# Forming 1 / (row sum of exponentials) as a power on GpSimd instead of a reciprocal on VectorE

## The chip, the cores and the metric

The kernel runs on one core of one Trainium2 chip. The core has five engines that run beside each other and meet only at semaphores: TensorE (PE, with its weight load PEld), VectorE (DVE), ScalarE (ACT), GpSimd (POOL) and SyncE (SP, which here only issues DMAs). The metric is the device time of one launch in microseconds; three runs of the kernel before took 1795.38 to 1799.1 us, median 1796.7.

## The reference

A gated cross attention is followed by a gated mixture of experts, for 8 batches of 512 tokens with 256 channels and a context of 1601 rows. What matters here is the attention. Its softmax runs over the query axis (`axis=2`), so each of the 1601 context rows is normalised over the 512 queries of its head:

```python
attn = jnp.einsum('bhnc,bhlc->bhnl', qh * scale, kh)
attn = jax.nn.softmax(attn, axis=2)
attn = attn / jnp.sum(attn, axis=-1, keepdims=True)
out = jnp.einsum('bhnl,bhlc->bhnc', attn, vh)
...
x = x + jnp.tanh(g_xattn[0]) * _L0_xattn_ref(_layernorm(x, axis=-1), ctx_1024, ctx_1024, ...)
x = x + jnp.tanh(g_ffn[0]) * _L0_ffn_ref(_layernorm(x, axis=-1), L0_ffn_router_w, L0_ffn_w1, L0_ffn_w2)
```

With the context rows on the partitions, the softmax's sum is a sum along a partition's own row, and its reciprocal can be multiplied into the values instead of into the probabilities.

## The kernel before

The attention goes batch by batch. A batch has 52 steps (`STEPS`): 4 groups of 4 heads, and for each group 13 tiles (`LT`) of 128 context rows (the last has 65). A step has two units of two heads. All 416 steps of the 8 batches do the same:

- TensorE makes the scores of a unit, two matmuls of 128x512 (`unit_scores`, line 732), into one of 3 slots of two PSUM banks. A slot is free again when ScalarE has done the exponentials of three units ago.
- VectorE takes the negated maximum over the queries (line 1114, one TENSOR_REDUCE per unit).
- ScalarE takes the exponentials, one ACTIVATE per head (line 934), and has their row sums written to `z`, 128x4 for a step, in a ring of 4 (`RING`). Its semaphore is `exp_done`.
- VectorE forms `rz` = 1 / `z` (`reciprocals`, line 1100). It does so for step s-1 behind the second maximum of step s.
- GpSimd multiplies the values of the step, a 128x4x17 tile (16 channels of 4 heads and a column of ones), with `rz` into `vz` (`weigh_values`, line 1337). In its program this stands at the head of step s for step s-1.
- TensorE multiplies `vz` with the exponentials into `acc` (`weigh`, line 745). In its program this stands three steps later (`LAG` = 3), between the scores of two units, so a late `vz` holds the scores behind it.

Each engine works through a fixed program in order. Around these steps a table, `FILL_AT`, places one "fill" at a step: the projections of the next batch, its layer normalisation, and the residual, normalisation and routing of the batch before (its "tail"). On GpSimd the fills are: for each chunk of the projected keys and queries, the middle part in the chunk's step (line 1389) and the low part one step later (line 1381); in steps 13 to 16 the tail's normalisation, `one_over_deviation` (lines 1306 and 1308) and six `by_row` (line 1314); in steps 17 to 20 the same for the next batch's input, with four `by_row`; and in steps 44 to 51 one indirect DMA each (line 1397). Chunks stand at steps 1, 3, 11, 13, 15, 17, 24, 26 (keys) and 30, 32 (queries). `one_over_deviation` has a power in it already: line 1308 raises a 128x4 tile to -1/2.

Batch 0 has no tail and batch 7 has no next batch. After the last batch, `last` goes on with the last routing, and some 500 us of expert blocks follow that neither form nor use `rz`. The profiled execution starts batch 4's exponentials at 634.5 us and those of batch 5 at 785.8 us; "step 13" below is step 13 of batch 4.

Of the kernel before, what the change touches and what calls it, by code (L numbers as in the profile page):

```python
# [207 lines left out]
def rows_of(lt):  # L208
    return min(P, L - lt * P)


def attention_and_routing(nc, ctx, block, keep, x, ctx_t, g_xattn, g_ffn, wq_t, wk_t, wv_t, wo_t, router_t,
# [8 lines left out]
    def sb(name, shape, dt=F32):  # L221
        return ctx.enter_context(nc.sbuf_tensor(name, shape, dt))
# [51 lines left out]
    rstd2 = sb("rstd2", [P, 2, NT])  # L274
    minus_half = sb("minus_half", [P, NT])
    prob = sb("prob", [P, 3, NT, E])
    one_hot = sb("one_hot", [P, 2, NT, E])
# [117 lines left out]
    ROUTE_STEPS, PLACE_STEPS = 25, 6  # L395
    DVE_SETUP = 7 + 2 * E

# [547 lines left out]
    def _(dve):  # L945
        for tile, value in ((v_ones[0][:, :, :, DH], 1.0), (v_ones[1][:, :, :, DH], 1.0), (vz[:, :, :, :], 0.0), (minus_half[:, :], -0.5),
                            (zero[:, :], 0.0), (seen[:, :], 0.0), (ones_e[:, :], 1.0)):
            dve.memset(tile, value).then_inc(dve_setup, 1)
# [146 lines left out]

        def reciprocals(b, s):

            r = rows_of(s % LT)
            dve.wait_ge(exp_done, 2 * (b * UNITS + 2 * s + 2))
            dve.reciprocal(rz[0:r, s % RING, :], z[0:r, s % RING, :]).then_inc(rz_ready, 1)  # L1100

        def take_acc(b, g):
# [3 lines left out]
        def run(it):  # L1106
            b = it.b
            for s in range(STEPS):
                for p in range(2):
# [9 lines left out]
                    if p == 1 and it.cur and s in (LT + LAG - 1, 2 * LT + LAG - 1, 3 * LT + LAG - 1):  # L1119
                        take_acc(b, s // LT - 1)  # L1120
                    if p == 1 and s == 0 and it.tail:
                        reciprocals(b - 1, STEPS - 1)
                    if p == 1 and s > 0 and it.cur:
                        reciprocals(b, s - 1)
                    f = it.fill(s)
# [36 lines left out]
        def last():  # L1162
            b = B - 1
            reciprocals(b, STEPS - 1)
            dve.wait_ge(last_router_summed, 1)
# [115 lines left out]
    def _(pool):  # L1281
# [48 lines left out]
        def weigh_values(b, s):  # L1330

            g, lt = s // LT, s % LT
            r = rows_of(lt)
            pool.wait_ge(rz_ready, b * STEPS + s + 1)

            wait(pool, pv_done, b * STEPS + s - RING + 1)
            pool.tensor_tensor(vz[0:r, s % RING, :, 0:DH + 1], v_ones[b % 2][0:r, lt, g * GH:(g + 1) * GH, :],  # L1337
                               rz[0:r, s % RING, :].unsqueeze(2).to_broadcast([r, GH, DH + 1]),
                               ALU.mult).then_inc(vz_ready, 1)
# [349 lines left out]
```

## Time and profile before

| | |
|---|---|
| runs | 1796.7, 1799.1, 1795.38 us |
| profiled execution, time | 1794.36 us |
| profiled execution, first to last instruction | 1792.6 us |
| granted TensorE clock, mean | 0.996 |
| busy: TensorE, VectorE, ScalarE, GpSimd | 1703.8, 1417.2, 1283.0, 538.2 us |

The span is first to last instruction; the time of the execution is 1.8 us longer. Engines are named PE, PEld, DVE, ACT, POOL and SP in the rows, and L1100 is line 1100 of the kernel. A group's row gives its busy time, the mean duration of one, then the idle time of the engine just ahead of these instructions with what ended it. Instructions overlap on an engine's pipeline: the start of the next can be earlier than the end of the one before, and what one costs in a full stretch is the distance from start to start.

### The profile page before, as it was taken

Reading aid. Unit: us, or ns where it says so; the run is one execution under the profiler, and the core shown is the slowest. Engines: PE = TensorE matmul, PEld = TensorE weight load, DVE = VectorE, ACT = ScalarE, POOL = GpSimd, SP = SyncE. Lnnn points to the kernel's source line nnn. Section 1 sums busy time; section 2 is a strip of 40 time slices with the busy share of each in tenths; the row PEclk is TensorE's granted clock in tenths of the full one; section 3 lists DMA queues with packets and bytes.
Section 4 is the critical chain, followed back from the end, with each engine's and each line's share of the span. In section 5 each row is a group of like instructions: output and inputs, shape, how many; then the busy total and the mean of one; then the engine's idle time right before and its main releaser. Section 6 shows DMA issues by size and latency. Waiting matters only on the chain.

```text
span 1792.6 us, 31795 instructions
## 1 busy us (share of the span) xinstructions
PE 1703.8 (95%) x10074; PEld 918.3 (51%) x10074; DVE 1417.2 (79%) x2293; ACT 1283.0 (72%) x3653; POOL 538.2 (30%) x821
## 2 busy tenths in 40 slices
PE   8999999999999999999999999889999999999997
PEld 5233334333333433333333342225899999999997
DVE  7998999999999999999999999997344444444442
ACT  5999999999999999999999999996111111111111
POOL 3331252352343225235223422213122222222222
PEclk9999999999999999999999999999999999999999
DMA  8546226414712721551371163419222222222221
GB/s 231 139 121 183 66 70 158 129 40 123 187 47 62 198 72 52 158 154 40 102 187 51 51 172 75 154 52 326 67 37 35 36 37 35 38 35 35 36 37 27
DMA packets 128247, 172.90 MB, mean 96 GB/s; under 512 B 14496, under 2 KB 105760, under 8 KB 128128
## 3 DMA queue, kind: packets, MB, share of 16 engines
q1 hardware_dynamic: 113152, 150.51, 30.8%
q0 software_dynamic: 14144, 20.44, 6.6%
q8 instruction: 54, 0.88, 0.2%
q14 instruction: 65, 0.53, 0.1%
q10 hardware_dynamic: 832, 0.53, 0.1%
HBM read 117.96 MB, written 53.47 MB: 96 GB/s over the span
## 4 chain that ended last, share of the span: by engine, by line
ACT 40%; PE 30%; DVE 20%; issue 7%; DMA 2%; POOL 1%; SPq 0%; POOLq 0%; DVEq 0%; ACTq 0%
ACT w_all L934 37%; DVE negmax L1114 14%; PE scores L1507 14%; PE scores L1520 13%; ACT w_all L879 1%; ACT parts L870 1%; DVE resid L1009 1%; DMA out<-row_t,gate_token 1%; PE spare L1497 1%; DVE rz L1100 1%; PE scores L732 1%; PE spare L593 1%; DVE x L1025 1%; DVE stats L1133 1%; DVE stats L1143 0%
## 5 line engine op out<-in xcount | busy, mean ns | idle before, releaser
L934 ACT ACTIVATE w_all<-scores,negmax 128x512 f32<-128x512 f32 (+1 forms) x1664 | 1128.9, 778 | 19.9 <-DVE negmax L1114 15.4
L1114 DVE TENSOR_REDUCE negmax<-scores 128x2 f32<-128x1024 f32 (+1 forms) x832 | 1001.9, 1215 | 53.8 <-PE scores L732 47.4
L732 PE MATMUL scores<-q_stack,w_all 128*128 128x512 bf16 (+1 forms) x1664 | 532.9, 385 | 42.1 <-ACT w_all L934 34.3
L934 ACT ACTIVATION_READ_ACCUMULATOR w_all<-scores,negmax 128x1 f32 (+1 forms) x1664 | 495.2, 298 | 0.0
L745 PE MATMUL acc<-w_all,vz 128*32 128x512 f32 (+1 forms) x3328 | 443.7, 605 | 0.0
L732 PEld LDWEIGHTS scores<-q_stack,w_all 128*128 128x128 bf16 (+1 forms) x1664 | 136.8, 99 | 575.2 <-ACT w_all L934 514.6
L1553 ACT ACTIVATE projections<-scores 128x512 f32<-128x512 f32 x142 | 84.8, 597 | 445.8 <-PE scores L1507 440.2
L1337 POOL TENSOR_TENSOR vz<-w_all,rz 128x68 f32<-128x68 f32 (+1 forms) x416 | 124.5, 299 | 776.3 <-DVE rz L1100 751.0
L1507 PEld LDWEIGHTS scores<-row_t,q_stack 128*128 128x128 f32 x2272 | 264.4, 192 | 7.0 <-issue 2.0
L1507 PE MATMUL scores<-row_t,q_stack 128*128 128x128 f32 x2272 | 265.6, 275 | 1.9 <-DVE row_t L1580 1.9
L1520 PE MATMUL scores<-room,projections 128*128 128x256 f32 x1136 | 256.8, 379 | 0.0
L1633 POOL DMA_INDIRECT out<-row_t,gate_token x71 | 120.3, 1694 | 407.9 <-DVE row_t L1593 374.3
L1520 PEld LDWEIGHTS scores<-room,projections 128*128 128x128 f32 x1136 | 210.4, 190 | 25.7
L1586 DVE COPY gate_token<-parts 128x2 f32<-128x2 f32 x71 | 12.0, 169 | 186.3 <-DMA out<-row_t,gate_token 186.3
L745 PEld LDWEIGHTS acc<-w_all,vz 128*32 128x32 f32 (+1 forms) x3328 | 65.6, 108 | 138.1 <-issue 121.9
L593 PE MATMUL spare<-w_all,projections 128*128 128x400 f32 (+1 forms) x228 | 97.7, 511 | 10.2 <-DVE resid L1009 10.2
L1593 DVE TENSOR_SCALAR row_t<-scores,gate_token 128x256 f32<-128x256 f32 x71 | 34.4, 484 | 88.0 <-PE scores L1520 88.0
L601 PE MATMUL spare<-projections,w_all 128*128 128x256 f32 (+1 forms) x400 | 103.1, 381 | 0.1
L1570 DVE COPY q_stack<-w_all 128x2048 f32 x71 | 86.9, 1225 | 6.4 <-issue 1.8
L1575 DVE COPY room<-w_all 128x2048 f32 x71 | 86.5, 1218 | 0.0
L601 PEld LDWEIGHTS spare<-projections,w_all 128*128 128x128 f32 (+1 forms) x400 | 73.6, 186 | 19.8 <-ACT w_all L879 3.3
L1100 DVE RECIPROCAL rz<-z 128x4 f32<-128x4 f32 (+1 forms) x416 | 69.7, 167 | 2.1 <-ACT w_all L934 2.1
(215 smaller groups left out, 1048.9 us busy)
## 6 DMA issues: line engine op xcount, KB each, us to landing
w_all<-k_parts SPq DMA_DIRECT2D x248, 200.1 KB, 3.5
w_all<-in_w SPq DMA_DIRECT2D x16, 1024.0 KB, 10.0
q_stack<-q_parts SPq DMA_DIRECT2D x248, 64.0 KB, 3.3
k_parts<-parts SPq DMA_DIRECT2D x42, 300.0 KB, 2.9
w_all<-in_ctx_t SPq DMA_DIRECT2D x7, 1601.0 KB, 7.1
parts<-routed SPq DMA_DIRECT2D x71, 129.0 KB
q_parts<-parts SPq DMA_DIRECT2D x14, 384.0 KB, 3.9
routed<-pad_row SPq DMA_DIRECT2D x8, 645.0 KB
```

The lines of the kernel that those rows point to most:

```text
L593: mm = pe.matmul(bank[:, 0:KCOLS[c + 1] - KCOLS[c]], wk_sb[:, k, m * P:(m + 1) * P], ctx_sb[:, k, KCOLS[c]:KCOLS[c + 1]], start=(k == 0), ...
L601: mm = pe.matmul(bank[0:r, (lt % 2) * D:(lt % 2 + 1) * D], ctx_sb[:, k, lt * P:lt * P + r], wv_sb[:, k, :], start=(k == 0), stop=(k == KC ...
L732: mm = pe.matmul(scores[0:r, 2 * (u % SLOTS) + j % 2, :], k_stacks[g][:, j, lt * P:lt * P + r], q_stack[:, g, j, :], start=True, stop=True)
L745: mm = pe.matmul(acc[32 * j:32 * j + 32, :], vz[0:r, s % RING, j, :], probs[0:r, s % RING, j, :], start=(lt == 0), stop=(lt == LT - 1))
L934: act.activation(probs[0:r, s % RING, j, :], scores[0:r, 2 * (u % SLOTS) + j % 2, :], ACT.Exp, bias=negmax[0:r, u % 4, j % 2:j % 2 + 1], a ...
L1100: dve.reciprocal(rz[0:r, s % RING, :], z[0:r, s % RING, :]).then_inc(rz_ready, 1)
L1114: dve.tensor_reduce(negmax[0:r, u % 4, :], scores[0:r, 2 * (u % SLOTS):2 * (u % SLOTS) + 2, :], AX.X, ALU.max, negate=True).then_inc(negma ...
L1337: pool.tensor_tensor(vz[0:r, s % RING, :, 0:DH + 1], v_ones[b % 2][0:r, lt, g * GH:(g + 1) * GH, :], rz[0:r, s % RING, :].unsqueeze(2).to_ ...
L1507: mm = pe.matmul(ps_hidden[:, slot * BANKS + h // HB, (h % HB) * BLK:(h % HB + 1) * BLK], w1_sb[:, slot, k * HID + h * P:k * HID + (h + 1) ...
L1520: mm = pe.matmul(ps_y[:, slot, 0:D], hidden[:, slot, h * BLK:(h + 1) * BLK], w2_sb[:, slot, h * D:(h + 1) * D], start=(h == 0), stop=(h == ...
L1570: dve.tensor_copy(w1_sb[:, slot, :], w1_all[:, bass.ds(e * (KC * HID), KC * HID)]).then_inc(w1_ready, 1)
L1633: pool.indirect_dma_start(out=out, out_offset=bass.IndirectOffsetOnAxis(gate_token[:, slot, 1:2].bitcast(U32), 0), in_=result[:, slot, :], ...
```

## The change

The power -1 of `z` is taken on GpSimd, with `tensor_tensor` and `ALU.pow` against a new 128x4 tile of -1, just ahead of the multiplication that uses it. `rz_ready`, which VectorE raised, is now raised by GpSimd and waited for by GpSimd itself. VectorE's `reciprocals` and its 415 calls inside the batches go; the last step of the last batch alone keeps a VectorE reciprocal, behind one added wait.

```diff
--- before.py
+++ after.py
@@ -273,6 +273,7 @@
     mv2 = sb("mv2", [P, NT, 2])
     rstd2 = sb("rstd2", [P, 2, NT])
     minus_half = sb("minus_half", [P, NT])
+    minus_one = sb("minus_one", [P, GH])
     prob = sb("prob", [P, 3, NT, E])
     one_hot = sb("one_hot", [P, 2, NT, E])
     tmp = sb("tmp", [P, 2, NT, E])
@@ -393,7 +394,7 @@
 
     passed_sp, passed_dve, passed_pool = (sem(f"passed_{e}") for e in ("sp", "dve", "pool"))
     ROUTE_STEPS, PLACE_STEPS = 25, 6
-    DVE_SETUP = 7 + 2 * E
+    DVE_SETUP = 8 + 2 * E
 
     def load_w1(eng, e):
         eng.dma_start(w1_all[:, e * KC * HID:(e + 1) * KC * HID].rearrange("p (k h) -> p k h", k=KC),
@@ -943,7 +944,7 @@
 
     @block.vector
     def _(dve):
-        for tile, value in ((v_ones[0][:, :, :, DH], 1.0), (v_ones[1][:, :, :, DH], 1.0), (vz[:, :, :, :], 0.0), (minus_half[:, :], -0.5),
+        for tile, value in ((v_ones[0][:, :, :, DH], 1.0), (v_ones[1][:, :, :, DH], 1.0), (vz[:, :, :, :], 0.0), (minus_half[:, :], -0.5), (minus_one[:, :], -1.0),
                             (zero[:, :], 0.0), (seen[:, :], 0.0), (ones_e[:, :], 1.0)):
             dve.memset(tile, value).then_inc(dve_setup, 1)
         for e in range(E):
@@ -1093,12 +1094,6 @@
             chain(dve.tensor_scalar(token[:, :], token[:, :], float(N), None, ALU.add))
             yield
 
-        def reciprocals(b, s):
-
-            r = rows_of(s % LT)
-            dve.wait_ge(exp_done, 2 * (b * UNITS + 2 * s + 2))
-            dve.reciprocal(rz[0:r, s % RING, :], z[0:r, s % RING, :]).then_inc(rz_ready, 1)
-
         def take_acc(b, g):
             dve.wait_ge(pv_done, b * STEPS + (g + 1) * LT)
             dve.tensor_copy(o_acc[:, :], acc[:, :]).then_inc(acc_taken, 1)
@@ -1118,10 +1113,6 @@
                         take_acc(b - 1, G - 1)
                     if p == 1 and it.cur and s in (LT + LAG - 1, 2 * LT + LAG - 1, 3 * LT + LAG - 1):
                         take_acc(b, s // LT - 1)
-                    if p == 1 and s == 0 and it.tail:
-                        reciprocals(b - 1, STEPS - 1)
-                    if p == 1 and s > 0 and it.cur:
-                        reciprocals(b, s - 1)
                     f = it.fill(s)
                     if f and f[0] not in ("v", "own_v", "x_turn") and p == (f[0] in ("q", "k")):
                         take(it, *f)
@@ -1161,7 +1152,10 @@
         dve.wait_ge(constants, 1)
         def last():
             b = B - 1
-            reciprocals(b, STEPS - 1)
+            dve.wait_ge(rz_ready, B * STEPS - 1)
+            dve.wait_ge(exp_done, 2 * B * UNITS)
+            r, at = rows_of(LT - 1), (STEPS - 1) % RING
+            dve.reciprocal(rz[0:r, at, :], z[0:r, at, :]).then_inc(rz_ready, 1)
             dve.wait_ge(last_router_summed, 1)
             dve.tensor_copy(router_sum[:, :], spare[:, 0:E]).then_inc(last_router_sum_taken, 1)
             dve.wait_ge(pv_done, B * STEPS)
@@ -1331,6 +1325,9 @@
 
             g, lt = s // LT, s % LT
             r = rows_of(lt)
+            if s < STEPS - 1 or b < B - 1:
+                pool.wait_ge(exp_done, 2 * (b * UNITS + 2 * s + 2))
+                pool.tensor_tensor(rz[0:r, s % RING, :], z[0:r, s % RING, :], minus_one[0:r, :], ALU.pow).then_inc(rz_ready, 1)
             pool.wait_ge(rz_ready, b * STEPS + s + 1)
 
             wait(pool, pv_done, b * STEPS + s - RING + 1)
```

On GpSimd, batch 1, from the end of step 12 to step 15 (65 rows is the last, short tile of a group; batches 2 to 6 have the same program). Before:

```order
L1337 TENSOR_TENSOR vz<-w_all,rz 65x4x17
L1306 TENSOR_SCALAR rstd<-mv 128x4
L1308 TENSOR_TENSOR rstd<-rstd,minus_half 128x4
L1314 TENSOR_TENSOR routed_rows<-x,mv 128x2x256
L1389 TENSOR_TENSOR parts<-resid,zero 128x401
L1337 TENSOR_TENSOR vz<-w_all,rz 128x4x17
L1314 TENSOR_TENSOR routed_rows<-x,mv 128x2x256
L1314 TENSOR_TENSOR routed_rows<-routed_rows,rstd 128x2x256
L1381 TENSOR_TENSOR parts<-resid,parts 128x401
L1337 TENSOR_TENSOR vz<-w_all,rz 128x4x17
```

and now:

```order
L1330 TENSOR_TENSOR rz<-z,minus_one 65x4
L1334 TENSOR_TENSOR vz<-w_all,rz 65x4x17
L1300 TENSOR_SCALAR rstd<-mv 128x4
L1302 TENSOR_TENSOR rstd<-rstd,minus_half 128x4
L1308 TENSOR_TENSOR routed_rows<-x,mv 128x2x256
L1386 TENSOR_TENSOR parts<-resid,zero 128x401
L1330 TENSOR_TENSOR rz<-z,minus_one 128x4
L1334 TENSOR_TENSOR vz<-w_all,rz 128x4x17
L1308 TENSOR_TENSOR routed_rows<-x,mv 128x2x256
L1308 TENSOR_TENSOR routed_rows<-routed_rows,rstd 128x2x256
L1378 TENSOR_TENSOR parts<-resid,parts 128x401
L1330 TENSOR_TENSOR rz<-z,minus_one 128x4
```

In the new rows L1330 is the power, L1334 the old L1337, L1300, L1302 and L1308 the old L1306, L1308 and L1314, and L1386 and L1378 the old L1389 and L1381. Each multiplication into `vz` has a power ahead of it, in the same place of the order; nothing else changed places.

On VectorE, batch 1, steps 11 to 13. Before:

```order
L1114 TENSOR_REDUCE negmax<-scores 65x2
L1143 BN_STATS stats<-room 128x6
L1114 TENSOR_REDUCE negmax<-scores 65x2
L1100 RECIPROCAL rz<-z 128x4
L1137 BN_AGGR mv<-stats 128x2 x4
L1114 TENSOR_REDUCE negmax<-scores 128x2
L1143 BN_STATS stats<-room 128x6
L1114 TENSOR_REDUCE negmax<-scores 128x2
L1100 RECIPROCAL rz<-z 65x4
L1009 SCALAR_TENSOR_TENSOR resid<-spare,parts 128x401
```

and now:

```order
L1109 TENSOR_REDUCE negmax<-scores 65x2
L1134 BN_STATS stats<-room 128x6
L1109 TENSOR_REDUCE negmax<-scores 65x2
L1128 BN_AGGR mv<-stats 128x2 x4
L1109 TENSOR_REDUCE negmax<-scores 128x2
L1134 BN_STATS stats<-room 128x6
L1109 TENSOR_REDUCE negmax<-scores 128x2
L1010 SCALAR_TENSOR_TENSOR resid<-spare,parts 128x401
```

L1109 is the old L1114, L1134 the old L1143, L1128 the old L1137 and L1010 the old L1009. The reciprocals are gone, and with each its wait for ScalarE; the rest stands as it stood.

## Rows read from the trace of the kernel before

**Rows 1.** The page: the chain that ended last, share of the span.
```profile
ACT 40%; PE 30%; DVE 20%; issue 7%; DMA 2%; POOL 1%; SPq 0%; POOLq 0%; DVEq 0%; ACTq 0%
```

**Rows 2.** The page, costliest groups: busy us, mean ns | idle before, releaser.
```profile
L934 ACT ACTIVATE w_all<-scores,negmax 128x512 f32<-128x512 f32 (+1 forms) x1664 | 1128.9, 778 | 19.9 <-DVE negmax L1114 15.4
L1114 DVE TENSOR_REDUCE negmax<-scores 128x2 f32<-128x1024 f32 (+1 forms) x832 | 1001.9, 1215 | 53.8 <-PE scores L732 47.4
...
L1337 POOL TENSOR_TENSOR vz<-w_all,rz 128x68 f32<-128x68 f32 (+1 forms) x416 | 124.5, 299 | 776.3 <-DVE rz L1100 751.0
...
L1100 DVE RECIPROCAL rz<-z 128x4 f32<-128x4 f32 (+1 forms) x416 | 69.7, 167 | 2.1 <-ACT w_all L934 2.1
```

**Rows 3.** Busy by stretch (from, to, length): PE, PEld, DVE, ACT, POOL; clock, DMA, GB/s.
```profile
632.00:781.00 149.00, 142.22 (x783) 50.94 (x783) 142.64 (x232) 146.34 (x431) 53.04 (x93) 1.00 0.39 109
674.50:692.80 18.30, 16.46 (x90) 5.58 (x93) 17.93 (x30) 17.72 (x53) 17.64 (x26) 1.00 0.20 66
```

**Rows 4.** Groups by form, ScalarE: steps 1 to 12 (two forms), then 24 to 51.
```profile
L934 ACT ACTIVATE w_all<-scores,negmax 128x512 f32<-128x512 f32 x45 | 30.3, 705 | 0.7 <-DVE negmax L1114 0.5
...
L934 ACT ACTIVATE w_all<-scores,negmax 65x512 f32<-65x512 f32 x4 | 2.7, 676 | 0.8 <-DVE negmax L1114 0.8
...
L934 ACT ACTIVATE w_all<-scores,negmax 128x512 f32<-128x512 f32 (+1 forms) x114 | 77.9, 810 | 0.0
```

**Rows 5.** Timeline, VectorE: start, us, engine, line; idle in brackets.
```profile
650.96 2.33 DVE L1114 TENSOR_REDUCE negmax<-scores 128x2 f32<-128x1024 f32 x2
653.21 0.17 DVE L1100 RECIPROCAL rz<-z 128x4 f32<-128x4 f32 x1
653.29 1.20 DVE L1114 TENSOR_REDUCE negmax<-scores 128x2 f32<-128x1024 f32 x1
...
701.62 1.23 DVE L1114 TENSOR_REDUCE negmax<-scores 128x2 f32<-128x1024 f32 x1 [0.20 <-PE scores L732]
```

**Rows 6.** Groups by form: the power of 128x4 on POOL, and the scatter.
```profile
L1397 POOL DMA_INDIRECT routed<-routed_rows,place x56 | 56.6, 1011 | 11.4 <-issue 11.4
...
L1308 POOL TENSOR_TENSOR rstd<-rstd,minus_half 128x4 f32<-128x4 f32 x16 | 16.6, 1038 | 1.3
```

**Rows 7.** Timeline, POOL, batch 4, from step 13.
```profile
674.51 0.30 POOL L1337 TENSOR_TENSOR vz<-w_all,rz 65x68 f32<-65x68 f32 x1 [1.71 <-DVE rz L1100]
674.77 0.23 POOL L1306 TENSOR_SCALAR rstd<-mv 128x4 f32<-128x4 f32 x1
675.08 1.04 POOL L1308 TENSOR_TENSOR rstd<-rstd,minus_half 128x4 f32<-128x4 f32 x1
676.21 1.04 POOL L1314 TENSOR_TENSOR routed_rows<-x,mv 128x512 f32<-128x512 f32 x1
677.20 0.85 POOL L1389 TENSOR_TENSOR parts<-resid,zero 128x401 bf16<-128x401 f32 x1
...
692.49 0.30 POOL L1337 TENSOR_TENSOR vz<-w_all,rz 128x68 f32<-128x68 f32 x1 [0.17 <-DVE rz L1100]
...
697.74 0.30 POOL L1337 TENSOR_TENSOR vz<-w_all,rz 128x68 f32<-128x68 f32 x1 [1.03 <-DVE rz L1100]
```

**Rows 8.** Timeline, ScalarE: last sum of step 12; one of step 23.
```profile
672.71 0.19 ACT L934 ACTIVATION_READ_ACCUMULATOR w_all<-scores,negmax 65x1 f32 x1
...
703.36 0.75 ACT L934 ACTIVATE w_all<-scores,negmax 128x512 f32<-128x512 f32 x1
```

**Rows 9.** Timeline, TensorE: weighing of steps 18 and 20, scores behind.
```profile
695.61 1.07 PE L745 MATMUL acc<-w_all,vz 128*32 128x512 f32 x8
...
699.98 1.06 PE L745 MATMUL acc<-w_all,vz 128*32 128x512 f32 x8
700.97 0.61 PE L732 MATMUL scores<-q_stack,w_all 128*128 128x512 bf16 x2
```

**Rows 10.** Busy by stretch, TensorE alone: length, busy; granted clock, DMA, GB/s.
```profile
1080.00:1088.60 8.60, 6.49 (x36) 1.00 0.37 95
1088.60:1092.00 3.40, 3.40 (x16) 0.50 0.96 253
```

## The prediction

> **What bounds the kernel now.** I read the chain of waits first, to see which engine sets the end. It gives ScalarE 40%, TensorE 30% and VectorE 20% of the span, GpSimd 1% [rows 1]; TensorE's share is largely the expert part. In the costliest groups the 1664 exponentials of ScalarE sat idle ahead for 19.9 us in all, 15.4 of it until VectorE's maxima [rows 2]. So in the attention ScalarE is nearly full, and no relief of VectorE can bring more than some 15 to 20 us. The reciprocals to be dropped are 416, 167 ns each, 69.7 us together [rows 2]. The busy time by stretch gives one batch: of 149.0 us ScalarE is busy 146.34, VectorE 142.64, GpSimd only 53.04 [rows 3]. The average hides what the second row of that group shows: from 674.5 to 692.8 us GpSimd is busy 17.64 of 18.30 us, with two normalisations and three key chunks in steps 13 to 18. That stretch comes in each of batches 1 to 6. ScalarE's groups by stretch show where it loses: 1.5 us (0.7 + 0.8) in steps 1 to 12, and nothing in steps 24 to 51 [rows 4].
>
> **What goes.** On VectorE a reciprocal costs less than its 167 ns, since it overlaps its neighbours: the second of a pair of maxima is over at 653.29, and the next begins there, with the reciprocal between; the pair without one between them took 2.33 us at 1.22 a piece, so one begins 0.11 us before the last ends [rows 5]. A reciprocal is thus worth 0.11 us of VectorE, 12 of them 1.3 us by step 12. ScalarE has 1.5 us of idle time to give back there, and part of that is held by TensorE or by a bank, not by VectorE. Bounds: 0 and 1.5 us a batch; I take 0.9, between them and nearer to the 1.3. From step 24 on ScalarE has no idle time, so the other 28 reciprocals bring nothing.
>
> **What comes.** 415 powers on GpSimd. The trace has the same operation on the same shape: line 1308, 128x4, 1038 ns, 16 times [rows 6]. In a full stretch it costs from its start at 675.08 to the next start at 676.21, which is 1.13 us [rows 7]. The scaling behind it keeps its 0.30 us, 0.26 from start to start (674.51 to 674.77), and so on an idle GpSimd `vz` is there 0.05 + 1.13 + 0.30 = 1.5 us behind the last row sum. At the head of the stretch the old path needed more: the sum ends at 672.90 [rows 8] and `vz` at 674.81 [rows 7], 1.9 us, since the reciprocal stood behind a maximum. Outside the full stretch I therefore cost the powers at nothing: a step lasts 2.87 us (149.0 / 52), and a power, a scaling and one chunk operation of 0.85 or 0.94 us are 2.3 us. With the scatter's 1.01 us in steps 44 to 51 [rows 6] they are 2.4 to 2.7 us. If that cover were gone, each step would run over by some tenths, which the three steps of lag absorb over 8 steps.
>
> The Trainium skill's Perfetto Trace Analysis (GPSIMD Engine Instruction) says not to trust the reported duration of a GpSimd instruction but the spacing of consecutive starts. Durations alone would make the seven powers below 0.6 us shorter a batch, some 4 us in all; the spacing in rows 7 is what I use.
>
> **The full stretch, step by step.** Step 12's last sum is there at 672.90 [rows 8]. Power 672.95 to 674.08, scaling to 674.34: line 1306 starts 0.43 us earlier than its 674.77 [rows 7]. From there GpSimd worked without a break up to 692.32 (692.49 less 0.17 of idle time), 17.55 us with five scalings in it. Five powers more are 5.65 us: it is done at 691.89 + 5.65 = 697.54. Then step 18: power to 698.67, `vz` at 698.97. A `by_row` of 0.99 from start to start (676.21 to 677.20), step 19 with 1.39, a `by_row`, and the power of step 20: 698.93 + 0.99 + 1.39 + 0.99 + 1.13 = 703.43, `vz` at 703.73. The row sums of these steps are no limit: step 20's scaling ran at 697.74 already [rows 7]. TensorE weighed step 18 at 695.61 and step 20 at 699.98 [rows 9]. So these come 3.4 and 3.8 us late. The other steps of the stretch end before that and are not added: lateness is one delay that grows.
>
> What of it reaches ScalarE: weighing at 703.78, scores 0.99 us later (699.98 to 700.97 [rows 9]), the maximum 0.65 us behind them (701.62 [rows 5]), 1.23 us for it, and the exponential at 706.7 us instead of 703.36 [rows 8]. That is +3.3 us. ScalarE has no idle time left afterwards to win it back. VectorE's 0.9 us moves the start of the whole sequence forward: +2.4 us a batch, and 6 x 2.4 = 14.4 us.
>
> Batches 0 and 7 have one normalisation each and no such stretch: at most a step is late by less than its slack. They keep VectorE's gain, which I put at 0.5 us for both. At the end of batch 7 the last power delays the weighing of step 50 by some 0.4 us, and the reciprocal kept on VectorE is where it was. The memset of the new tile lies ahead of the first data, nothing. Sum: 14.4 - 0.5 + 0.4 = +14.3 us. On the profiled execution's 1794.4 us (span 1792.6 and 1.8 around it) that is 1808.7; it lies 2.3 us under the median of the runs, 1796.7, and on the median it is **1811 us**, 0.8% slower.
>
> Bounds of the sum: with 1.00 us a power instead of 1.13 (a pipelined start) the lateness shrinks by 0.9, with VectorE's full 1.5 it shrinks by 0.6 more: +0.9 a batch, 1802. With nothing from VectorE and half a microsecond lost while the pipeline refills, +3.8 a batch, 1820.
>
> **Rivals.**
> 1. *The price of the power is the tile's size, and no backlog forms.* Then only VectorE's relief is left: 6 x 0.9 to 1.5 us and a little from batches 0 and 7, some 9 us: 1788. For it: 128x4 has a 17th of the elements of the scaling, which takes 0.30 us. Against it: line 1308, 16 times at 1038 ns. The Trainium skill's GPSIMD Engine Reference (Performance versus the Vector engine) gives a two-input tensor_tensor 2.6 cycles an element at 1.2 GHz; an estimate from that page for 4 elements is 9 ns on top of a fixed part, which would make this rival true. The trace does not agree where the operation is a power. It ends on the faster side if seven powers add less than some 1.3 us a batch, that is under 0.2 us each.
> 2. *The slack takes it.* TensorE is late, but scores already made feed ScalarE through, and VectorE's gain covers the rest: 1797, within 3.6 us. For it: three slots of scores. Against: the slack from maximum to exponential behind step 20's weighing is about half a microsecond, which the path above already spends.
> 3. *TensorE's clock falls in the gap.* Where the trace shows a stretch of 8.6 us with 6.49 busy, the clock granted afterwards was 0.50 for 3.4 us, which is 1.2 GHz [rows 10]. A hole of 3 us in steps 18 to 20 leaves a thinner stretch than that. In that slow stretch TensorE was busy all of 3.40 us [rows 10]; work that takes half of that at full clock is late by some 1.3 us on top, 8 us over six batches: 1819.
> 4. *GpSimd stays behind.* The backlog meets the chunks at steps 24 and 26 before it is gone, or the low parts of a chunk reach SyncE so late that ScalarE waits for a free buffer: 1 to 2 us more a batch, 1823.
>
> **How the numbers follow.** Forecast 0.60, rival 1 0.07, rival 2 0.09, rival 3 0.15, rival 4 0.09. What a measurement can tell from no change is about 0.2%, 3.6 us: 1793.1 to 1800.3. Rival 1 is the faster side with 0.07, and 0.02 of the forecast's lower end; rival 2 and 0.02 of the lower end fall within; the rest is slower: 0.09, 0.10, 0.81. The range leaves out rival 1, most of rival 2 and the far end of 4: 1799 to 1825.
>
> **What would show it.** In the profile after: the power's group on GpSimd with 415 at about 1040 ns; GpSimd busy about 107 us of a batch; VectorE's reciprocals gone and its busy time down by 69 us. TensorE's weight load for `acc` waits for `vz`, which it did for 16 us in all, with 3 us and more at a time, around steps 18 to 20 of batches 1 to 6 alone. ScalarE has an idle time of about 3 us there. A batch of 1 to 6 lasts 151.3 + 2.4 = 153.7 us from its first exponential to the next batch's (785.8 - 634.5 = 151.3 now); batches 0 and 7 stay as they are. It is wrong if batches 1 to 6 don't grow, if the waits lie in other steps, or if the clock shows 0.50 in these stretches.

## The result, and the profile after

The changed kernel took 1827.28 us (median of six runs, 1819.88 to 1829.52) against 1797.64 of the kernel before (1795.38 to 1799.1): the ratio is 1.0158, with a 95% interval of 1.0143 to 1.0173. It is slower by twice what was forecast, and 2.3 us above the range. The profiled execution took 1826.45 us with a span of 1824.7, 32.1 us more than the span before.

The page after, the chain that ended last and the groups that answer to [rows 1] and [rows 2]:

```profile
PE 41%; ACT 28%; POOL 11%; DVE 11%; issue 7%; DMA 2%; POOLq 0%; SPq 0%; DVEq 0%; ACTq 0%
...
L935 ACT ACTIVATE w_all<-scores,negmax 128x512 f32<-128x512 f32 (+1 forms) x1664 | 1128.7, 772 | 43.3 <-DVE negmax L1109 41.0
L1109 DVE TENSOR_REDUCE negmax<-scores 128x2 f32<-128x1024 f32 (+1 forms) x832 | 998.0, 1217 | 96.5 <-PE scores L733 87.1
L1330 POOL TENSOR_TENSOR rz<-z,minus_one 128x4 f32<-128x4 f32 (+1 forms) x415 | 421.1, 1015 | 354.7 <-ACT w_all L935 334.7
...
L746 PE MATMUL acc<-w_all,vz 128*32 128x512 f32 (+1 forms) x3328 | 449.1, 612 | 17.6 <-POOL vz L1334 17.5
...
L1334 POOL TENSOR_TENSOR vz<-w_all,rz 128x68 f32<-128x68 f32 (+1 forms) x416 | 125.8, 302 | 32.7
```

GpSimd was 1% of the chain and is 11% now. The power is 415 times 1015 ns; 1040 was forecast. ScalarE's idle time ahead of its exponentials has grown from 19.9 to 43.3 us, still until the maxima. VectorE lost 415 of its 416 reciprocals, which took 69.7 us together, but what it gained is idle time: it waits 96.5 us ahead of its maxima, mostly for scores, where it waited 53.8. The scaling starts at once (32.7 us of idle time ahead of it in place of 776.3); the power took over the wait.

By stretch (from, to, length, then PE, PEld, DVE, ACT, POOL, the granted clock, DMA, GB/s), batches 4 and 5 from their first exponential to the next batch's, to be set beside the first of [rows 3]:

```profile
648.70:807.70 159.00, 148.04 (x793) 52.80 (x792) 143.83 (x182) 149.51 (x436) 107.26 (x147) 0.97 0.36 103
807.70:962.90 155.20, 143.71 (x797) 50.96 (x800) 143.58 (x183) 149.05 (x437) 107.37 (x147) 1.00 0.39 105
```

GpSimd is busy 107 us of a batch, as forecast. The batches last 159.0 and 155.2 us; before, each of batches 1 to 6 lasted 151.3. So equal programs now have unequal lengths, and the longer one has the lower mean clock. Below, a batch's length is taken so from the starts of the exponentials, and "+3.8" is what it lasts over 151.3.

| batch | 1 | 2 | 3 | 4 | 5 | 6 |
|---|---|---|---|---|---|---|
| over 151.3 us | +3.8 | +6.2 | +4.6 | +7.8 | +3.9 | +6.2 |
| TensorE at clock 0.50 near 61 us into it | 0 | 6.8 | 3.4 | 10.2 | 0 | 6.8 |

Batches 0 and 7 changed by +0.2 and +0.1 us; in both profiles the clock fell for 3.4 us where batch 7 starts. Near 46 us the clock also fell in batch 1, for 3.4 us, which that batch's length doesn't show. Three things are in this table: a part that every batch has, and which stands at +2.7 at step 32; +0.31 and +0.75 us more at steps 33 and 34 of every batch (the shift of the exponentials from the start of the step to its end, against the kernel before); and the clock.

**The wait that was forecast.** GpSimd in batch 5 (start, us, line), the powers and scalings of steps 17, 18 and 20, which answer to [rows 7]:

```profile
867.01 1.02 POOL L1330 TENSOR_TENSOR rz<-z,minus_one 128x4 f32<-128x4 f32 x1
868.11 0.30 POOL L1334 TENSOR_TENSOR vz<-w_all,rz 128x68 f32<-128x68 f32 x1
...
870.27 1.01 POOL L1330 TENSOR_TENSOR rz<-z,minus_one 128x4 f32<-128x4 f32 x1
871.36 0.30 POOL L1334 TENSOR_TENSOR vz<-w_all,rz 128x68 f32<-128x68 f32 x1
...
874.96 1.01 POOL L1330 TENSOR_TENSOR rz<-z,minus_one 128x4 f32<-128x4 f32 x1
876.04 0.30 POOL L1334 TENSOR_TENSOR vz<-w_all,rz 128x68 f32<-128x68 f32 x1
```

and TensorE's weighings of the same steps, which answer to [rows 9]:

```profile
868.47 1.06 PE L746 MATMUL acc<-w_all,vz 128*32 128x512 f32 x8 [1.32 <-POOL vz L1334]
869.47 0.60 PE L733 MATMUL scores<-q_stack,w_all 128*128 128x512 bf16 x2
...
871.71 1.07 PE L746 MATMUL acc<-w_all,vz 128*32 128x512 f32 x8 [0.40 <-POOL vz L1334]
872.71 0.60 PE L733 MATMUL scores<-q_stack,w_all 128*128 128x512 bf16 x2
...
876.40 1.06 PE L746 MATMUL acc<-w_all,vz 128*32 128x512 f32 x8 [0.31 <-POOL vz L1334]
877.40 0.61 PE L733 MATMUL scores<-q_stack,w_all 128*128 128x512 bf16 x2
```

A power costs 1.08 to 1.10 us from its start to its scaling's. Each weighing begins 0.35 to 0.36 us behind the start of its scaling: `vz` is what TensorE waits for. The scores follow 1.00 us later. Step 20 is weighed 68.7 us into the batch; before it was 65.5 (699.98 less 634.5), and the forecast was 69.3. The waits begin with step 17 here and with step 15 in batch 4 (0.34 us); forecast were steps 18 to 20. The longest wait of all batches, that of a weight load, is 2.6 us, where 3 and more was forecast.

**The clock.** TensorE alone in batch 4 (length, busy, granted clock, DMA, GB/s), to be set beside [rows 10]:

```profile
706.00:710.50 4.50, 2.38 (x17) 1.00 0.00 0
710.50:720.80 10.30, 10.30 (x41) 0.50 0.09 31
720.80:724.00 3.20, 3.20 (x17) 1.00 0.00 0
```

and its timeline around the change of clock:

```profile
704.79 1.06 PE L746 MATMUL acc<-w_all,vz 128*32 128x512 f32 x8 [0.78 <-POOL vz L1334]
...
709.39 1.07 PE L746 MATMUL acc<-w_all,vz 128*32 128x512 f32 x8 [2.12 <-POOL vz L1334]
710.39 0.94 PE L733 MATMUL scores<-q_stack,w_all 128*128 128x512 bf16 x2
...
713.64 1.94 PE L746 MATMUL acc<-w_all,vz 128*32 128x512 f32 x8
```

A wait of 0.78 us for `vz` ended at 704.79. The next, of 2.12 us, left TensorE busy for 2.38 of 4.50 us; then it was granted 0.50, its lower level of 1.2 GHz, for 10.2 us. The weighing took 1.94 us there in place of 1.07.

**The held instruction.** VectorE in batch 5, at steps 33 and 34:

```profile
903.51 0.77 DVE L970 TENSOR_TENSOR one_hot<-tmp,top 128x32 f32<-128x32 f32 x1
904.20 1.21 DVE L1109 TENSOR_REDUCE negmax<-scores 128x2 f32<-128x1024 f32 x1
...
908.95 1.12 DVE L1062 TENSOR_SCALAR top<-top,tgf 128x4 f32<-128x4 f32 x1
909.98 1.21 DVE L1109 TENSOR_REDUCE negmax<-scores 128x2 f32<-128x1024 f32 x1
```

GpSimd at the same time:

```profile
903.06 1.17 POOL L1378 TENSOR_TENSOR parts<-resid,parts 128x512 bf16<-128x512 f32 x1
...
908.88 1.16 POOL L1378 TENSOR_TENSOR parts<-resid,parts 128x512 bf16<-128x512 f32 x1
```

The multiplication `top<-top,tgf` takes 1.12 us and ends at 910.07, 0.03 behind the low part of the query chunk on GpSimd. `one_hot<-tmp,top` takes 0.77 us and ends at 904.28, 0.05 behind the other low part. Before, the same two on VectorE:

```profile
878.79 0.42 DVE L969 TENSOR_TENSOR one_hot<-tmp,top 128x32 f32<-128x32 f32 x1
...
884.03 0.20 DVE L1061 TENSOR_SCALAR top<-top,tgf 128x4 f32<-128x4 f32 x1
```

and the low parts on GpSimd:

```profile
878.01 1.16 POOL L1381 TENSOR_TENSOR parts<-resid,parts 128x512 bf16<-128x512 f32 x1
...
884.46 1.16 POOL L1381 TENSOR_TENSOR parts<-resid,parts 128x512 bf16<-128x512 f32 x1
```

There they took 0.42 and 0.20 us. The second was over before the low part began. The first was held already: it ends at 879.21, 0.04 behind the low part, and in e4_no_recip below, with nothing of GpSimd's beside it, it takes 0.18. The power has moved the low parts against VectorE's program.

The power itself held nothing here. The next product in the changed kernel's VectorE program, with both inputs in SBUF, begins 0.52 us into a power and takes 0.15 us:

```profile
911.11 0.15 DVE L1064 TENSOR_TENSOR top<-top 128x8 f32<-128x8 f32 x1
```

```profile
910.59 1.01 POOL L1330 TENSOR_TENSOR rz<-z,minus_one 128x4 f32<-128x4 f32 x1 [0.55 <-ACT w_all L935]
```

What holds VectorE stands behind it: the low parts, and the scaling too (`tmp<-prob,top` of step 30 took 0.18 us before and takes 0.32 beside one).

### The profile page after: what moved, and what is told of

It reads as the page before. It is cut to its first block, busy times and chain, and to the rows that moved or that the text cites. A ratio compares the mean times of both kernels' runs of the same rounds, so it can differ in the third digit from the quotient of the medians.

```text
span 1824.7 us, 31811 instructions
## 1 busy us (share of the span) xinstructions
PE 1716.5 (94%) x10074; PEld 922.7 (51%) x10074; DVE 1403.8 (77%) x1879; ACT 1287.6 (71%) x3653; POOL 960.0 (53%) x1236
## 4 chain that ended last, share of the span: by engine, by line
PE 41%; ACT 28%; POOL 11%; DVE 11%; issue 7%; DMA 2%; POOLq 0%; SPq 0%; DVEq 0%; ACTq 0%
ACT w_all L935 26%; PE scores L1504 13%; PE scores L1517 13%; DVE negmax L1109 7%; PE acc L746 5%; PE scores L733 5%; POOL rz L1330 4%; POOL routed_rows L1308 2%; PE spare L679 1%; ACT w_all L880 1%; POOL vz L1334 1%; DVE resid L1010 1%; DMA out<-row_t,gate_token 1%; PE spare L1494 1%; POOL parts L1386 1%
## 5 line engine op out<-in xcount | busy, mean ns | idle before, releaser
L935 ACT ACTIVATE w_all<-scores,negmax 128x512 f32<-128x512 f32 (+1 forms) x1664 | 1128.7, 772 | 43.3 <-DVE negmax L1109 41.0
L1109 DVE TENSOR_REDUCE negmax<-scores 128x2 f32<-128x1024 f32 (+1 forms) x832 | 998.0, 1217 | 96.5 <-PE scores L733 87.1
L1330 POOL TENSOR_TENSOR rz<-z,minus_one 128x4 f32<-128x4 f32 (+1 forms) x415 | 421.1, 1015 | 354.7 <-ACT w_all L935 334.7
L935 ACT ACTIVATION_READ_ACCUMULATOR w_all<-scores,negmax 128x1 f32 (+1 forms) x1664 | 484.0, 291 | 0.0
L746 PE MATMUL acc<-w_all,vz 128*32 128x512 f32 (+1 forms) x3328 | 449.1, 612 | 17.6 <-POOL vz L1334 17.5
L1334 POOL TENSOR_TENSOR vz<-w_all,rz 128x68 f32<-128x68 f32 (+1 forms) x416 | 125.8, 302 | 32.7
```

The lines of the kernel that those rows point to most:

```text
L746: mm = pe.matmul(acc[32 * j:32 * j + 32, :], vz[0:r, s % RING, j, :], probs[0:r, s % RING, j, :], start=(lt == 0), stop=(lt == LT - 1))
L935: act.activation(probs[0:r, s % RING, j, :], scores[0:r, 2 * (u % SLOTS) + j % 2, :], ACT.Exp, bias=negmax[0:r, u % 4, j % 2:j % 2 + 1], a ...
L1109: dve.tensor_reduce(negmax[0:r, u % 4, :], scores[0:r, 2 * (u % SLOTS):2 * (u % SLOTS) + 2, :], AX.X, ALU.max, negate=True).then_inc(negma ...
L1330: pool.tensor_tensor(rz[0:r, s % RING, :], z[0:r, s % RING, :], minus_one[0:r, :], ALU.pow).then_inc(rz_ready, 1)
```

## The experiments

The numbers of batches below are from one profiled execution each; ratios are against the kernel before on the same chip (medians of it 1794.0, 1794.1 and 1792.7 us in the three groups of runs).

### Where the powers stand: outside and inside the full stretch

A step's power is on GpSimd where `on_pool` says so, else its reciprocal on VectorE as before.

```diff
+    def on_pool(b, s):          # e1_outside
+        return (b, s) != (B - 1, STEPS - 1) and not (1 <= b <= 6 and 12 <= s <= 20)
+    def on_pool(b, s):          # e2_inside
+        return 1 <= b <= 6 and 12 <= s <= 20
...
+            if on_pool(b, s):
+                pool.wait_ge(exp_done, 2 * (b * UNITS + 2 * s + 2))
+                pool.tensor_tensor(rz[0:r, s % RING, :], z[0:r, s % RING, :], minus_one[0:r, :], ALU.pow).then_inc(pow_done, 1)
```

> Powers on GpSimd everywhere but in steps 12 to 20 of batches 1 to 6; there VectorE keeps its reciprocals. Theory A (the time goes in the full stretch of GpSimd, steps 13 to 20, by late values and the clock that falls in the gap; apart from it, 1.1 us a batch at steps 33 and 34, where a small VectorE multiplication is held behind a GpSimd instruction): steps 13 to 23 are as before, the clock stays at 1.00 in them, the shift at steps 33 and 34 stays: about +0.8 us a batch, +5 us, 1802 to 1804. Rival B (the power's longer latency costs a little everywhere): most of the 30 us stays, above 1815. Rival C (all of it is the stretch): 1793 to 1797.

Measured: 1800.11 us, ratio 1.0037 (1.0023 to 1.0051). Each of batches 1 to 6 is +0.73: -0.38 by step 32, +0.35 at step 33 and +0.75 at step 34. No clock of 0.50 in them.

> The other half: powers on GpSimd only in steps 12 to 20 of batches 1 to 6, reciprocals on VectorE elsewhere. Theory A: +3.1 us a batch at full clock, up to +7 where the clock falls to 0.50, nothing at steps 33 and 34: 1816 to 1824. Rival B: nine of 52 powers give a sixth of the loss, 1802. Rival C: all of it, 1827.

Measured: 1817.56 us, ratio 1.0125 (1.0104 to 1.0146). The batches are +5.3, +6.9, +3.7, +3.0, +6.9 and +3.8, with 6.8, 10.2, 3.4, 0, 10.2 and 3.4 us at clock 0.50 near 61 us; nothing at steps 33 and 34.

So 54 of the 415 powers carry the wait and the clock's part, and the other 361 carry the two held instructions. The batch of +3.0 has no fall near 61 us, but one of 3.4 us near 46, as batch 1 of the changed kernel has. Without a fall near 61, 3.0 and 0.73 make 3.7, about the changed kernel's 3.8.

### Reciprocals kept, powers added

```diff
+            if (b, s) != (B - 1, STEPS - 1):
+                pool.wait_ge(exp_done, 2 * (b * UNITS + 2 * s + 2))
+                pool.tensor_tensor(unused[0:r, s % RING, :], z[0:r, s % RING, :], minus_one[0:r, :], ALU.pow).then_inc(pow_done, 1)
+                pool.wait_ge(pow_done, b * STEPS + s + 1)
             pool.wait_ge(rz_ready, b * STEPS + s + 1)
```

> VectorE keeps every reciprocal and the values are scaled with them; GpSimd takes the power of the same sums as well, into a tile that nobody reads. GpSimd has the load of the change, VectorE is not relieved. Theory A: the loss is GpSimd's load, so it is that of the changed kernel plus the 0.4 us a batch that VectorE's relief gave: 1826 to 1833. Rival D (the loss came with the altered order, since VectorE no longer waits for ScalarE): 1797 to 1803.

Measured: 1823.77 us, ratio 1.0160 (1.0139 to 1.0181), as the changed kernel's 1.0158. Two batches without any fall of the clock are +3.9: +3.48 by step 32 and +0.43 at steps 33 and 34. The changed kernel stands at +2.73 at step 32 of its batches 1 and 5. The wait alone is thus worth 3.48 us, and VectorE's relief 0.75. The relief is missing here, yet the kernel isn't slower than the changed one: the reciprocals keep VectorE's program where the gate's multiplication of step 33 takes 0.20 us, and step 34 adds 0.05 us in place of 0.75.

### No power at all, and a cheap one

```diff
-                pool.tensor_tensor(rz[0:r, s % RING, :], z[0:r, s % RING, :], minus_one[0:r, :], ALU.pow).then_inc(rz_ready, 1)
+                pool.tensor_tensor(rz[0:r, s % RING, :], z[0:r, s % RING, :], minus_one[0:r, :], ALU.mult).then_inc(rz_ready, 1)   # e8_cheap
```

In e4_no_recip the whole step goes, and `rz` is set once to 0.002.

> No reciprocal anywhere: the values are scaled with a constant 0.002 instead of 1 / (row sum), GpSimd waits for ScalarE alone. It shows what VectorE's relief alone is worth. Theory A (most of the relief turns into waiting for a free bank, since three slots hold VectorE back): 0.3 to 0.6 us a batch, 1793 to 1796. Rival E (the prediction's 0.9 us a batch or more, hidden in the changed kernel): 1788 to 1791.

Measured: 1789.73 us, ratio 0.9975 (0.9966 to 0.9985). The batches are -0.67 (-0.44 by step 15, -0.76 by step 21), but for two with 3.4 us at clock 0.50 near 46 us, which are +0.97.

> The changed kernel, with a multiplication by -1 in the place of each power, same tiles, same place: the values are scaled with minus the sum instead of its reciprocal. Theory A (the loss is the 1.1 us that a power takes, seven of them behind each other): a 128x4 multiplication takes about 0.25 us, the stretch ends in time, batches at -0.4 us and at most the shift at steps 33 and 34: 1792 to 1799 on a before of 1796. Rival H (any second instruction with its own wait on GpSimd costs so much): above 1810.

Measured: 1791.43 us, ratio 0.9984 (0.9975 to 0.9994); five batches are -0.38, with +0.37 at step 34, and the sixth, with 3.4 us at clock 0.50 near 46 us, is +1.25. The page has the operation in the power's place:

```profile
L1109 DVE TENSOR_REDUCE negmax<-scores 128x2 f32<-128x1024 f32 (+1 forms) x832 | 997.2, 1218 | 69.3 <-PE scores L733 59.4
...
L1330 POOL TENSOR_TENSOR rz<-z,minus_one 128x4 f32<-128x4 f32 (+1 forms) x415 | 83.6, 202 | 624.9 <-ACT w_all L935 596.5
```

The same instruction form on the same shape takes 202 ns as a multiplication and 1015 as a power. The 0.8 us between them decide the sign of the change. The most that dropping the reciprocals can bring is e4_no_recip's 0.25%, and the rest of VectorE's freed time goes into waiting for scores (69.3 us in place of 53.8).

### The held instruction at step 34

The kernels so far already show the price of the gate's multiplication, `top<-top,tgf`. In e8_cheap it begins 0.45 us into the low part, takes 0.74 us and ends 0.02 us behind it:

```profile
882.91 0.74 DVE L1062 TENSOR_SCALAR top<-top,tgf 128x4 f32<-128x4 f32 x1
```

```profile
882.46 1.17 POOL L1378 TENSOR_TENSOR parts<-resid,parts 128x512 bf16<-128x512 f32 x1
```

It takes 0.45, 0.74 and 1.12 us in e4_no_recip, e8_cheap and the changed kernel, and step 34 adds 0.09, 0.37 and 0.75 us: one for one.

Three kernels try to move it away in different ways. The first folds it into the next instruction, and its control does so in the kernel before:

```diff
-            chain(dve.tensor_scalar(top[:, 7, :], top[:, 7, :], tgf[:, 0:1], None, ALU.mult))
-            yield
-            chain(dve.tensor_tensor(top[:, 4:6, :], top[:, 0:2, :],
-                                    top[:, 7, :].unsqueeze(1).to_broadcast([P, 2, NT]), ALU.mult))
+            chain(dve.scalar_tensor_tensor(out=top[:, 4:6, :], in0=top[:, 0:2, :], scalar=tgf[:, 0:1],
+                                           in1=top[:, 7, :].unsqueeze(1).to_broadcast([P, 2, NT]),
+                                           op0=ALU.mult, op1=ALU.mult))
```

> The changed kernel, with the routing's small multiplication by the gate (a tensor_scalar of 128x4 in SBUF, 1.12 us in each of six batches where it took 0.20 before) folded into the next instruction. Theory A (VectorE waited there for GpSimd's 1.16 us instruction to end, 1.13 us a batch at steps 33 and 34): this shift goes, 6.8 us less than the changed kernel, ratio to before about 1.012. Rival F (the shift at steps 33 and 34 has another cause, for example a late TensorE): it stays, ratio 1.016.

> The kernel before with the same folding, as a control: one VectorE instruction of 0.2 us less a batch, where ScalarE has no idle time. Both theories: no difference, within 1 us of before.

Measured: 1822.94 us, ratio 1.0159 (1.0142 to 1.0177), and 1795.17, ratio 1.0002 (0.9993 to 1.0012). The shift at step 34 stayed at +0.75, so folding took nothing away. In the control the clock fell for 3.4 us near 46 us in two of the six batches, at 1.6 us each: those falls come without any late `vz` and aren't the change's. On VectorE the folded instruction stands in the same place:

```profile
909.38 1.12 DVE L1062 SCALAR_TENSOR_TENSOR top<-top,tgf 128x8 f32<-128x8 f32 x1
```

and GpSimd beside it:

```profile
909.32 1.16 POOL L1377 TENSOR_TENSOR parts<-resid,parts 128x512 bf16<-128x512 f32 x1
```

It is held as its forerunner was, to 0.02 us behind GpSimd's end. What counts is the place in the order, not the operation. The next two change what stands there. One computes only 8 of the 512 columns of that low part in batches 1 to 6; the other puts an empty turn ahead of the multiplication, so that it comes one maximum later.

```diff
+                    if (name, i) == ("q", 1) and b > 0:      # e9_short_low
+                        n = 8
                     pool.tensor_tensor(parts[:, c % 2, 2, 0:n], resid[:, at % 2, 0:n], parts[:, c % 2, 1, 0:n],
                                        ALU.subtract).then_inc(parts_ready, 1)
...
+            yield                                            # e10_turn
             chain(dve.tensor_scalar(top[:, 7, :], top[:, 7, :], tgf[:, 0:1], None, ALU.mult))
```

> The changed kernel, where GpSimd forms only 8 of the 512 columns of the low part of the second query chunk, in step 33 of batches 1 to 6 (the rest keeps what stood there). Theory A (the VectorE instruction of step 33 that reads SBUF is held until GpSimd's 1.16 us instruction ends): it takes 0.2 to 0.4 us instead of 1.12, and the 1.13 us at steps 33 and 34 go, 6.8 us less than the changed kernel, ratio about 1.012. Rival F (the cause is not this instruction): the shift stays.

Measured: 1824.72 us, ratio 1.0163 (1.0136 to 1.0190). VectorE and, in the second fence, GpSimd:

```profile
913.11 0.22 DVE L1062 TENSOR_SCALAR top<-top,tgf 128x4 f32<-128x4 f32 x1
```

```profile
913.05 0.20 POOL L1380 TENSOR_TENSOR parts<-resid,parts 128x8 bf16<-128x8 f32 x1
```

The multiplication takes 0.22 us and the +0.75 at step 34 is gone from all six batches; the +0.31 at step 33 stays. The expected ratio of 1.012 was missed: this kernel's clock fell in all six batches of its profile (6.8, 10.2, 6.8, 6.8, 10.2 and 3.4 us), and the interval is as wide as the gain.

> The changed kernel with an empty turn in VectorE's routing ahead of the gate's multiplication, so that this and what follows stand one unit of two heads later, away from GpSimd's 1.16 us instruction, but beside the power of step 33. Theory A: at most a power's 1.0 us can hold it there; the shift at steps 33 and 34 falls from 1.13 to between 0 and 0.5 us, 4 to 7 us less than the changed kernel. Rival F: the shift stays at 1.13.

Measured: 1819.2 us, ratio 1.0150 (1.0133 to 1.0166). VectorE and GpSimd:

```profile
904.16 0.22 DVE L1063 TENSOR_SCALAR top<-top,tgf 128x4 f32<-128x4 f32 x1
```

```profile
902.96 1.16 POOL L1379 TENSOR_TENSOR parts<-resid,parts 128x512 bf16<-128x512 f32 x1
```

The low part is whole here, and the multiplication begins behind its end (904.12) and takes 0.22 us. The +0.75 is gone, and three batches without a fall of the clock are +2.9 in place of +3.8. In both kernels the low part's overlap was taken away, once by its length and once by the order, and the delay went with it: within a batch it is shown. In the kernel's whole time, 1.0150 against 1.0158, the intervals overlap, and the gain doesn't show.

### The clock

Transposes of no use keep TensorE at work while it waits for `vz`: 10 ahead of the weighings of steps 16 to 19, or 5 ahead of those of steps 17 and 18, in batches 1 to 6.

```diff
+            if behind is not None and 1 <= b <= 6 and 17 <= s <= 18:      # e11_warm5; e7_warm: 16 to 19
+                pe.wait_ge(exp_done, 2 * (b * UNITS + behind - SLOTS) + 1)
+                keep_warm(scores[:, 2 * (behind % SLOTS), :], TURNS)      # 5; e7_warm: 10
             pe.wait_ge(vz_ready, b * STEPS + s + 1)
```

> The changed kernel, with 10 transposes of a constant ahead of the weighing of steps 16 to 19 in batches 1 to 6, into a score bank that is free and written again afterwards: TensorE works where it waited for late values. Theory A (a part of the loss, 9 us in the profile, is the clock at 0.50 behind the gap): no fall of the clock at 61 us into a batch, every batch at about +3.9 us, 5 to 9 us less than the changed kernel, ratio about 1.012. Rival G (the clock is not what costs, the batches differ by the transfers of the chunks): batches still differ by up to 4 us, ratio 1.016 or, by the added work, more.

Measured: 1822.88 us, ratio 1.0163 (1.0146 to 1.0180). No clock of 0.50 near 61 us, but the batches are +5.1 (two, with 3.4 us at 0.50 near 46 us, +5.9): 40 transposes cost about what the clock would have.

> As with ten transposes, but five, ahead of the weighing of steps 17 and 18 alone, which is where TensorE waited 0.8 and 2.1 us. Theory A: less work is added, the clock stays at 1.00 behind 61 us of a batch, and batches 1 to 6 all take +3.9 to +4.4 us: 3 to 8 us less than the changed kernel, ratio 1.012 to 1.014. Rival G: the batches without a fall of the clock cost as much as those with it, ratio 1.016.

Measured: 1813.68 us, ratio 1.0117 (1.0100 to 1.0134). All six batches are +3.82 to +3.84 and none falls near 61 us. Batch 4 by stretch:

```profile
645.30:800.40 155.10, 142.29 (x792) 52.08 (x808) 143.64 (x182) 149.43 (x437) 107.26 (x147) 1.00 0.37 105
```

and TensorE's timeline in the place where the clock had fallen:

```profile
703.69 0.71 PE L609 MATMUL scores<-ident,ones 128*128 128x128 f32 x5
705.98 1.07 PE L750 MATMUL acc<-w_all,vz 128*32 128x512 f32 x8 [1.58 <-POOL vz L1338]
```

`vz` is as late as before (the weighing begins 60.7 us into the batch in both), and TensorE still waits 1.58 us for it. Only 0.71 us of transposes fill the gap, the clock stays at 1.00, and the unequal lengths are gone. Against the changed kernel this is 0.41% or 7.4 us (the two intervals make that uncertain by about 4); the six batches of the changed kernel's profile are together 9.3 us above six times 3.83.

### The powers where there is room

```diff
+    def on_pool(b, s):
+        return b < B and s < 12
```

> Powers on GpSimd in steps 0 to 11 of every batch alone, reciprocals on VectorE elsewhere, so that neither the full stretch nor step 33 has any. Theory A: each batch gains the 0.35 us of steps 1 to 12 and loses nothing: 0 to 3 us less than before, which is hardly to be told; if the clock falls at 46 us into a batch, as it did in some batches of other kernels, 1.6 us of loss for each. Rival I (any power costs): 3 us or more above before.

Measured: 1791.51 us, ratio 0.9991 (0.9982 to 1.0001): no difference that can be told. Three batches are -0.38; three have 3.4 us at clock 0.50 near 46 us and are +1.2. The relief of the first 12 steps is real and small, and this doesn't beat the kernel before.

## Why the prediction was wrong

The terms of the sum, in us, forecast and as measured in the profiles:

| term | forecast | measured |
|---|---|---|
| stall behind the full stretch | 6 x 3.3 = 19.8 | 6 x 3.48 = 20.9 (e3_both) |
| VectorE's relief | -6 x 0.9 = -5.4 | -6 x 0.75 = -4.5 (3.48 less 2.73) |
| held VectorE instructions | 0 | 6 x (0.31 + 0.75) = 6.4 |
| TensorE's clock | 0 (a rival) | 9.3 |
| batches 0 and 7 | -0.5 | +0.3 |
| ahead of batch 0 and behind batch 7 | +0.4 | -0.5 |
| sum | +14.3 | +31.9, of 32.1 |

**Right.** The power's price was the row of line 1308: 1015 ns against 1038, and 1.08 to 1.10 us from start to start against 1.13. The Trainium skill's GPSIMD Engine Reference (Performance versus the Vector engine) counts two-input operations by the element, which made rival 1; 1015 ns for the power and 202 for the multiplication on the same 4 elements a partition show that the operation sets the price here. The place of the stall, steps 17 to 20 of batches 1 to 6, was right but for the first waits, and its size to 0.2 us. VectorE's relief was near in size and wrong in place: all of it was to come by step 12, and by then the batches stand at -0.32; in e4_no_recip more than half comes in steps 12 to 20. That the size is near is luck. Three slips of the working changed little. The path from step 12 to step 20 holds nine powers, not seven, so the lower bound's price of 1.00 us takes 1.2 us off a batch, not 0.9. Half of 3.40 us at the low clock is 1.7, not 1.3. And rival 2 with the forecast's lower end makes 0.11, not 0.10.

**Wrong, first: "Outside the full stretch I therefore cost the powers at nothing."** That step counted GpSimd's time and found slack, and there was slack: `vz` comes in time in those steps. It did not look at who else is touched when GpSimd's own instructions move. In steps 33 and 34 the low parts came to lie over two small VectorE instructions that read SBUF. By their ends VectorE is held until GpSimd's instruction is over; from step 24 on ScalarE has no idle time, so VectorE's delay passes to it through the maxima. For `top<-top,tgf` (0.75 us a batch) e9_short_low and e10_turn show it. For `one_hot<-tmp,top` (0.31 us) it is argued: in e1_outside, e3_both, e5_fold_after, e7_warm, e9_short_low, e10_turn and e11_warm5 its longest takes 0.70 to 0.77 us and step 33 is late, in e2_inside and e12_early it takes 0.42, in e4_no_recip and e8_cheap 0.18, and step 33 isn't; no run moved it alone. The Trainium skill says as much in SBUF — State Buffer (SBUF: two separate sides): VectorE and GpSimd share a port pair that one of them holds for a whole instruction while the other is blocked, for VectorE's instructions with two SBUF inputs or in a 2-port mode. The ends 0.02 to 0.05 us behind the low parts' agree with that; whether the multiplication ran in such a mode no trace tells. For the power the trace does not agree: 43 `tensor_tensor` of VectorE with both inputs in SBUF begin inside one in the changed kernel, and they take 0.15 to 0.18 us. Nor does every hold cost time: `prob<-prob,top` in step 26 went from 0.18 to 0.57 us beside a low part, and the shift of the exponentials of steps 24 to 30 varies by no more than 0.04. The prediction did not weigh the shared ports, though they speak against this change, and the text ahead of it is wrong where it lets the engines meet only at semaphores.

**Wrong, second: the clock stood among the rivals.** Rival 3 had a chance of 0.15 as if it were another outcome. It is one more term on top of the forecast's own wait, and it needed only that wait. Its size was off in two ways. The low clock lasted 6.8 or 10.2 us in three of four falls, not 3.4. And a fall of 3.4 us behind the wait cost 0.7 us, not 1.3, one of 6.8 us 2.3 and one of 10.2 us 3.9 (changed kernel, batches 3, 2 and 4, less 3.83). Near 46 us, in kernels without the wait, 3.4 us cost 1.5 to 1.6 (e4_no_recip, e6_fold_before, e8_cheap, e12_early). With its measured prices the forecast and rival 3 together would have given about 1820, and with the held instructions 1827.

**The other rivals.** Rival 1 is refuted by 1015 ns, and e8_cheap shows that it would have come true with a cheap operation: 0.9984. Rival 2 is refuted: in batch 5 step 20 is weighed 3.2 us late, and 2.7 of it reach ScalarE. Of rival 4 one ingredient is there. ScalarE in batch 5:

```profile
859.50 0.50 ACT L871 ACTIVATE parts<-spare 128x400 bf16<-128x400 f32 x1 [2.04 <-DMA k_parts<-parts]
```

It waits 2.04 us for a buffer that a transfer to memory still held. But that batch is +3.85, as are the batches of e11_warm5 with far less of that wait (+3.82 to +3.84): the delay only comes earlier, and the later wait for `vz` is shorter by it (1.32 us in place of 2.12). It adds nothing.

**A sign that was stated wrongly.** VectorE's busy time was to fall by 69 us; it fell by 13.4 (1417.2 to 1403.8). Busy time counts a moment once however many instructions overlap in it, so a reciprocal between two maxima held 0.11 us of it at most, which the prediction had worked out itself. With neither reciprocals nor powers (e4_no_recip) it is 1397.8, 19.4 less than before; the changed kernel's longer holds put some of that back. TensorE's waits for `vz`, 16.2 us before, are these now (weight load, then matmul: us, times, longest), more and longer as forecast:

```profile
PEld acc L746 <- POOL vz L1334: 62.4, 148, 2.6
...
PE acc L746 <- POOL vz L1334: 17.5, 18, 2.1
```

**Open.** What decides whether the clock falls in a batch: the program is the same in batches 1 to 6, yet it fell in 4 of 6 here, in 5, 3 and 6 of 6 in e2_inside, e3_both and e9_short_low. The length of the wait doesn't decide it: batches 1 and 3 of e10_turn and 2 and 5 of e3_both wait 2.12 us in the same place as the falling ones, and don't fall. Where it had fallen near 46 us into a batch, it never fell again near 61 (batch 1 here, one batch each of e2_inside, e3_both and e5_fold_after). The wait at 61 us is shorter there, 1.5 to 1.8 us, but no run tried it. What makes it fall near 46 us, in kernels with and without powers, is open too.

## What to carry to other kernels

An operation moved to an idle engine moves every instruction behind it there; cost the stretch where that engine is full, by starts, and then look at which small VectorE instructions on SBUF come to lie beside GpSimd's long ones. A wait of TensorE for a late operand (up to 2.1 us without a matmul here) can have a second price, the clock: it belongs in the sum, with a range, not among the alternatives. And relief for an engine is worth what the engine it feeds sits idle for, here 0.25% for all 415 reciprocals.

## What the runs showed of the hardware

- On GpSimd a `tensor_tensor` of 128x4 takes 1015 ns as a power and 202 ns as a multiplication; the power is 1.08 to 1.10 us from start to start.
- A VectorE instruction of 0.20 us on 128x4 in SBUF, begun 0.07 us behind a GpSimd subtraction of 1.16 us, took 1.12 us; a `tensor_tensor` of 0.18 us took 0.42 in the kernel before and 0.77 in the changed one, each time until 0.04 to 0.05 us behind GpSimd's end. The maxima, which read PSUM, kept their 1.2 us beside GpSimd.
- A power of 1.01 us held nothing: a `tensor_tensor` with both inputs in SBUF, begun 0.52 us into it, took 0.15 us.
- After 4.50 us with 2.38 busy TensorE was granted 0.50 for 10.2 us; 0.71 us of transposes ahead of each of two weighings kept 1.00. A fall behind a wait cost 0.7 of 3.4 us to 3.9 of 10.2; one of 3.4 us with no late `vz` about cost 1.5 to 1.6.
